# Eleven steps instead of seven fetched row by row by SyncE, six single-row DMAs a group, in a graph edge-convolution kernel

## What is computed

```python
x_src, x_dst = x[src], x[dst]
theta_x = (x_dst - x_src) @ theta_w.T + theta_b
phi_x = x_src @ phi_w.T + phi_b
e = relu(theta_x + phi_x)
out = segment_max(e, dst, num_segments=6250)      # 0 where a node has no edge
return layernorm(x + where(isfinite(out), out, 0))
```

## Time and profile before

| | |
|---|---|
| median of 3 runs | 1034.67 us (1034.25 to 1035.08) |
| the profiled execution | 1036.28 us, span 1034.5 us |
| busy PE / DVE / ACT / POOL | 837.8 / 693.0 / 336.8 / 771.0 us |
| gathers of POOL in the main loop (L465) | 684, 966 ns each |
| single-row DMAs of SP (L383) | 896 |
| mean granted clock of PE | 0.923 |

### The profile page before, as it was taken

One profiled execution on the slowest core, in us unless ns is written; L12 is line 12 of the kernel. 1 busy time (PEld: TensorE's weight loads), 2 busy tenths in 40 slices (PEclk: granted clock), 3 DMA queues, 4 the chain that ended last, 5 costly groups with the idle time before them and its releaser, 6 DMA issues. The chain is left out here.

```text
span 1034.5 us, 15863 instructions
## 1 busy us (share of the span) xinstructions
PE 837.8 (81%) x3875; PEld 437.8 (42%) x3875; DVE 693.0 (67%) x1732; ACT 336.8 (33%) x701; POOL 771.0 (75%) x793
## 2 busy tenths in 40 slices
PE   5976899999999999999999999999998946650000
PEld 5832444445444544454445444454443335440000
DVE  6734666766767767676766767767765546565698
ACT  3921233333333333233333333333221121110366
POOL 6877777777777777777777777777777777775773
PEclk9988999999999999999999999999998969885555
DMA  8955667687777777767777777777866789974365
GB/s 273 368 179 179 219 221 238 220 267 228 240 243 239 248 233 240 250 221 254 236 243 241 245 240 239 231 253 233 263 221 223 231 276 311 283 239 161 117 203 177
DMA packets 116641, 243.80 MB, mean 236 GB/s; under 512 B 19632, under 2 KB 57733, under 8 KB 116549
## 3 DMA queue, kind: packets, MB, share of 16 engines
q1 hardware_dynamic: 78244, 138.69, 37.5%
q0 software_dynamic: 37728, 103.04, 34.7%
q10 hardware_dynamic: 576, 1.06, 0.3%
HBM read 127.29 MB, written 115.45 MB: 235 GB/s over the span
## 5 line engine op out<-in xcount | busy, mean ns | idle before, releaser
L465 POOL DMA_INDIRECT rows<-b_table,idx x684 | 660.6, 966 | 208.5 <-issue 176.2
L639 PE MATMUL ps_a<-work,shared 128*128 128x512 bf16 x2940 | 667.1, 382 | 37.8 <-DVE work L819 37.0
L639 PEld LDWEIGHTS ps_a<-work,shared 128*128 128x128 bf16 x2940 | 281.3, 98 | 386.2 <-DVE work L819 47.7
L549 ACT COPY hist<-acc 128x512 f32<-128x512 f32 x253 | 148.7, 588 | 489.2 <-DVE hist L863 488.9
L863 DVE SCALAR_TENSOR_TENSOR acc<-hist,reset,rows 128x256 f32<-128x256 f32 x154 | 76.1, 494 | 195.3 <-issue 157.3
L819 DVE TENSOR_SCALAR work<-batch,node 128x512 bf16<-128x512 int16 x490 | 161.5, 373 | 6.2 <-PE ps_a L639 6.2
L863 DVE SCALAR_TENSOR_TENSOR acc<-acc,reset,rows 128x256 f32<-128x256 f32 x253 | 124.7, 493 | 49.4 <-DMA rows<-b_table,idx 36.8
L863 DVE SCALAR_TENSOR_TENSOR hist<-acc,reset,rows 128x256 f32<-128x256 f32 x253 | 122.3, 484 | 27.3 <-DVE acc L863 1.8
L700 PE MATMUL ps_a<-theta_sb,shared 128*128 128x256 f32 x196 | 56.9, 446 | 36.2 <-DVE shared L909 27.5
L451 POOL DMA_INDIRECT early<-in_x,idx_first x51 | 58.7, 1150 | 17.7 <-issue 15.2
L700 PEld LDWEIGHTS ps_a<-theta_sb,shared 128*128 128x128 f32 x196 | 41.7, 223 | 51.4 <-issue 44.7
(11 more groups left out here) (129 smaller groups left out, 481.2 us busy)
## 6 DMA issues: line engine op xcount, KB each, us to landing
runmax<-hist SPq DMA_DIRECT2D x260, 384.0 KB, 3.1
direct<-b_table SPq DMA_DIRECT2D x896, 1.0 KB
rows<-b_table,idx POOLq DMA_INDIRECT x684, 3.5
b_table<-rows SPq DMA_DIRECT2D x7, 896.0 KB, 7.4
shared<-in_xt SPq DMA_DIRECT2D x49, 128.0 KB, 4.4
early<-in_x SPq DMA_DIRECT2D x12, 512.0 KB
out<-hist SPq DMA_DIRECT2D x11, 512.0 KB, 3.3
hist<-in_xt SPq DMA_DIRECT2D x7, 512.0 KB, 7.9
```

The lines of the kernel that those rows point to most:

```text
L465: pool.indirect_dma_start(out=rows[:, PLACE[k], :], out_offset=None, in_=b_table, in_offset=bass.IndirectOffsetOnAxis(ap=idx[:, k:k + 1], ...
L549: nc.scalar.copy(hist[:, slot:slot + n - 1, :], acc[:, at:at + n - 1, :]).then_inc(s_copied, 1)
L639: mm = pe.matmul(ps_a[banks(b)[k]][:].rearrange("p j d -> p (j d)"), split[:, part, t, k * P:(k + 1) * P], hot[:, i % HOT, :], start=(t == ...
```

## The change

Three numbers are changed, nothing else: which groups begin with a step that SP fetches, and how many rows SP issues after each group's write.

```diff
-DIRECT_GROUPS = (35, 69, 98, 130, 162, 194, 226)
+DIRECT_GROUPS = (26, 45, 66, 89, 109, 130, 154, 174, 194, 216, 238)
 DIRECT_SLOTS = 3
-ROWS_A_GROUP = 4
+ROWS_A_GROUP = 6
```

## The result

| | before | changed |
|---|---|---|
| median | 1034.46 us (4 runs) | 1081.63 us (4 runs, 1079.24 to 1082.73) |
| ratio | 1 | 1.0455, 95% interval [1.0433, 1.0478] |
| span of the profiled run | 1034.5 us | 1080.9 us |
| gathers in the main loop, first and last start | 684, 78.6 to 945.3 us | 680, 79.7 to 993.0 us |
| last row DMA of SP, start | 820.0 us | 927.4 us |

The changed kernel is 4.5% slower. The forecast was 1108 us, 1062 to 1153: the measured time lies inside, 26 us under the forecast, and the sign is the forecast one.

What follows compares the result with a forecast made beforehand. POOL's gathers were taken to bound the kernel before, SP's issuing after: SP done at 953.2 us, plus 3.6 and 62.2, last gather at 1019.0, span 73.7 longer; 1036.3 + 73.7 − 1.6 = 1108 us, range 1062 to 1153.

Steps and rivals of the forecast that it cites:

- POOL bounds the loop before, a gather is worth 1.27 us: Main loop: POOL issues 684 gathers, one every 1.269 us; four fewer save 5.1 us if POOL stays the bound.
- SP's work no longer fits, VectorE waits in two places, POOL for it: Main loop from about group 8: SP needs 3.68 us a group, POOL 3.31; VectorE waits for `hist` writes and direct rows.
- The sum of SP's work, 865.6 us: SP's queue through group 234: writes 192.7, pitches 524.3, register loads 129.8, other issues 10.1, late tiles and pairs 8.7 us.
- From SP's last row to the end: After group 234: 3.6 us for the last direct rows' landing and folds, then 62.2 us to the last gather's start.
- The pull of the small packets: DMA engines: 512 added row DMAs at about 16 packets each, 41 us of each engine, costed at nothing.
- TensorE's clock: Rival, chance 0.12: stalls at direct groups halve TensorE's granted clock and TensorE takes over the loop; 1135 us.
- the hidden SP: Rival, chance 0.03: SP's added work is hidden and POOL sets the end, four gathers earlier; 1029.6 us, faster.

Runs made afterwards that it cites:

- the split with eleven steps: Changed kernel, but ScalarE issues the last 32 of each direct step's 128 rows, SP the first 96; 1033.5 us, ratio 0.9968; on the slow chip 1427.1 us.
- no reloads: Changed kernel, but SP loads row numbers into its registers once instead of 44 times; 1030.3 us, ratio 0.9964.
- loads of 16: Changed kernel, but row numbers loaded 16 at a time instead of 32; 1108.0 us, ratio 1.0727; on the slow chip 1546.8 us.
- five rows, nine steps: Changed kernel, but five rows a group instead of six and nine direct groups instead of eleven; 1031.05 us, ratio 0.998.
- the run with the later groups: Changed kernel, but its direct groups come nine groups after their last row instead of three; 1075.9 us, ratio 1.0423.

## Why the prediction was right

*POOL bounds the loop before, a gather is worth 1.27 us.* Right. In the kernels in which POOL stays the bound and has no late step, gathers follow each other every 1.27 us as before, (939.0 − 76.2)/679 in the split with eleven steps. By their ratios they gained 2.1 us (two gathers fewer), 3.7 and 3.3 us (four fewer) and 5.3 us (five fewer), about 1 us a gather; the four intervals are wide and all hold 1.27.

*SP's work no longer fits, VectorE waits in two places, POOL for it.* Right, by the rows above and by the experiments. The three ways of taking work from SP (no reloads, fewer rows a group, a second queue) each gave the time back, and the one that added work (loads of 16) lengthened it by just that. Two details were off: VectorE waited for `direct` at ten of the eleven places, not at the first, and up to 13.2 us where some 10 were named.

*The sum of SP's work, 865.6 us.* This is the mis-sized term. SP began at 87.2 us and was through at 927.6 us: 840.4 us, less 6.2 us of waits, 834 us. Of the 31 us too many, 129.8 − 110.6 = 19 us are the register loads, and if the rest of the sum is right the remaining 12 us make the pitch (from one row to the next) 0.437 instead of 0.447 us (12/1173 = 0.010); read off directly it is 0.435 us over 1144 pairs. A start 1.1 us later and 6.2 us of waits where 1.5 were put in took 6 us of the error back, so that SP was through 25.6 us early; the time was 26 us under the forecast. Why a load costs less in the changed kernel, the timelines of SP show when one sorts the loads by how many rows stand between the write of the maxima and the load (means in us, worked out from the single instructions):

| loads | right behind the write | 1 row | 2 rows | 3 rows | 4 rows |
|---|---|---|---|---|---|
| before, 32 | 2.96 (28) | | | | |
| changed, 32 | 2.89 (15) | | 2.47 (15) | | 2.16 (14) |
| five rows, nine steps, 32 | 2.88 (8) | 2.88 (7) | 2.42 (7) | 2.21 (7) | 2.16 (7) |
| loads of 16 | 1.89 (30) | | 1.52 (29) | | 1.25 (29) |

With four rows a group and 32 numbers a load, every load of the kernel before fell right behind a write, so its trace had only the dearest place. With six, a third do. The second row behind a write is dear too: 0.48 us from the second row's issue to the third's, 0.42 to 0.43 us everywhere else. Rows five and six, which the change adds, are of the cheap kind. The mean over the old positions was thus above what the added rows cost. I had the common pack's value of 0.44 before me and chose the mean.

*From SP's last row to the end.* 3.6 + 62.2 us from there to the last gather's start were predicted, 993.0 − 927.6 = 65.4 us measured. Right.

*The pull of the small packets.* Costed at nothing, and the split with ScalarE, which has the same 1408 rows, bears it out. But my count of 16 packets a row was wrong: queue q1 has 79281 packets instead of 78244, 1037 more for 512 rows, so two a row. The cost that was left out would have been some 5 us of each DMA engine, not 41. The 9616 packets under 512 B belonged for the most part to other DMAs.

```profile
q1 hardware_dynamic: 79281, 139.22, 36.2%
```

*TensorE's clock.* It fell, behind direct stalls: PE stood for 9.85 us before 318.9 us. In the stretch from 316 to 326 us the granted clock was 0.71 in the mean, and between 319 and 321 us, with PE at work again, it was at the lower level, 0.50.

```profile
318.89 5.29 PE L639 MATMUL ps_a<-work,shared 128*128 128x512 bf16 x17 [9.85 <-DVE work L819]
```

```profile
316.00:326.00 10.00, 7.11 (x27) 3.46 (x29) 8.83 (x23) 3.41 (x7) 7.56 (x9) 0.71 0.69 217
```

It did not decide: SP waited for copies only 6.2 us in all, so VectorE and PE held it up nowhere for long. The run with the later groups settles it: without the direct stalls the clock stays up, 0.99 from 104 to 830 us where the changed kernel had 0.96, and the time is 1075.9 us all the same.

```profile
104.00:830.00 726.00, 669.87 (x3122) 328.48 (x3183) 463.15 (x1229) 221.39 (x451) 524.49 (x547) 0.99 0.70 224
```

Of the rivals, the hidden SP would have needed a pitch under 0.38 us; the trace has 0.437.

## What to carry to other kernels

Work moved to a queue that computes nothing is not free: its issue time adds up, and the question is whether the sum per loop turn stays under that of the engine which sets the pace; here it did at five rows a turn and did not at six, and on one chip it did not at five either. Such a queue is read from its waits: as long as they are spread over the whole loop, it has room, and the sum of these waits is all there is of it. And a mean price from the trace is the price at the places where the instructions stood: when a change puts them elsewhere, sort the rows by what stands before them first.

## What the runs showed of the hardware

- A load of SP's registers takes 2.9 us for 32 and 1.9 us for 16 right behind a 384 KB write issued on the same queue, 2.16 and 1.25 us when four single-row DMAs stand between. By these a register costs 0.06 us and the rest, 0.9 us behind the write and 0.3 us four rows later, falls with the distance from the write; whether the time or the rows between count was not separated.
- A single-row DMA of 1 KB whose address comes from a register takes SP 0.41 to 0.48 us from one to the next, 0.23 us of it the DMA instruction.
- On one chip the same program took 1375 us instead of 1034; the traces of two other kernels there have gaps of about 0.70 us between SP's instructions.
